# A GNN layer's row fetches: SP takes one tile of 48 by byte addresses, in loops of three ring rounds

## The reference

```python
h = relu(layernorm(x))                                        # 12,500 x 256, the "nodes" below
sender_features = nodes[senders]                              # one row of h for each edge
msg_in = jnp.concatenate([sender_features, edges], axis=-1)   # 256 + 64 columns
messages = msg_in @ W_message
agg = jax.ops.segment_sum(messages, receivers, num_segments=total_nodes)
h1 = _layer_norm(jax.nn.relu(agg) + nodes, ln_aggr_scale, ln_aggr_bias)
nodes_out = _relu_mlp_skip(h1, [mlp_W0, mlp_W1, mlp_W2], [mlp_b0, mlp_b1, mlp_b2])
out = x + _layer_norm(nodes + nodes_out, ln_out_scale, ln_out_bias)
```

## Time and profile before

| | |
|---|---|
| Median of 3 runs (lowest, highest) | 2134.97 us (2129.38, 2136.38) |
| The profiled execution, its span | 2135.35 us, 2133.5 us |
| Busy share of PE, PEld, DVE, ACT, POOL | 75%, 52%, 45%, 19%, 74% |
| Mean granted TensorE clock | 0.905 of full speed |
| Edge loads from SP: number, size, to landing | 206, 256 KB, 6.0 us |

### The profile page before, as it was taken

The page is one execution under the profiler, slowest core; times in us unless marked ns, Lnnn a source line. Parts: engine busy times, 40 slices in busy tenths (PEclk is TensorE's granted clock), DMA queues, the critical chain, the costliest instruction groups (busy, mean ns, idle before and its releaser), DMA issues.

```text
span 2133.5 us, 41823 instructions
## 1 busy us (share of the span) xinstructions
PE 1609.0 (75%) x6722; PEld 1119.5 (52%) x6723; DVE 967.5 (45%) x4162; ACT 408.4 (19%) x1209; POOL 1572.2 (74%) x1645
## 2 busy tenths in 40 slices
PE   0059796697778769769769787878887887878886
PEld 0047574475456557547546555545555554545554
DVE  7866453353344344335335334434343434433445
ACT  5852111121111111111111111111111111111112
POOL 7657777777777777777777777777777777777772
PEclk9989997898888889879889889999999999999988
DMA  9796466556646646655664664665566466566461
GB/s 384 249 247 187 139 174 166 142 163 171 166 135 174 166 137 176 165 152 155 168 165 143 165 169 135 172 166 158 146 173 162 138 168 163 145 165 163 140 188 55
DMA packets 369326, 357.18 MB, mean 167 GB/s; under 512 B 256288, under 2 KB 312672, under 8 KB 369152
## 3 DMA queue, kind: packets, MB, share of 16 engines
q0 software_dynamic: 78576, 214.67, 35.3%
q1 hardware_dynamic: 233984, 89.44, 17.1%
q10 hardware_dynamic: 56592, 51.54, 7.7%
HBM read 329.01 MB, written 26.48 MB: 167 GB/s over the span
## 4 chain that ended last, share of the span: by engine, by line
POOL 42%; SPq 23%; issue 21%; PE 7%; DVE 2%; DMA 2%; ACT 2%; DVEq 0%; POOLq 0%; ACTq 0%
POOL ring L435 42%; SPq L401 16%; SPq L327 4%; PE acc_banks L628 3%; SPq L342 2%; ACT xs L761 1%; SPq L328 1%; PE agg_bank L504 1%; DMA xs<-x 1%; PE agg_bank L509 1%; PE y_bank L492 1%; DVE x_stats L1042 1%; ACT ring L761 1%; PE z_bank L492 1%; POOL xs L447 0%
## 5 line engine op out<-in xcount | busy, mean ns | idle before, releaser
L435 POOL DMA_INDIRECT ring<-h_table,src_all x1557 | 1491.7, 958 | 488.1 <-issue 471.8
L628 PE MATMUL acc_banks<-ring,onehot 128*128 128x320 f32 x3290 | 1027.4, 463 | 330.6 <-DMA ring<-h_table,src_all 161.2
L628 PEld LDWEIGHTS acc_banks<-ring,onehot 128*128 128x128 f32 x3290 | 634.2, 201 | 683.7 <-issue 487.7
L1159 DVE TENSOR_SCALAR onehot<-iota,dst_rel 128x128 f32<-128x128 f32 x1664 | 350.2, 296 | 353.0 <-PE acc_banks L628 325.4
L825 DVE TENSOR_TENSOR visit_rows<-agg_bank,visit_rows 128x256 f32<-128x256 f32 x98 | 41.6, 424 | 722.9 <-PE agg_bank L509 715.2
L678 ACT ACTIVATE uT<-z_bank,fp 128x128 f32<-128x128 f32 x196 | 78.9, 453 | 1266.4 <-PE z_bank L498 1261.5
L504 PE MATMUL agg_bank<-wm,ST 128*128 128x256 f32 (+1 forms) x582 | 172.0, 418 | 0.0
L504 PEld LDWEIGHTS agg_bank<-wm,ST 128*128 128x128 f32 (+1 forms) x582 | 110.7, 203 | 59.6 <-issue 40.0
L498 PE MATMUL z_bank<-ident,z 128*128 128x128 f32 x196 | 41.6, 297 | 104.5 <-DMA ring<-h_table 103.5
L684 ACT ACTIVATE r_bank<-y_bank,fp 128x128 f32<-128x128 f32 x196 | 58.6, 337 | 297.8 <-PE y_bank L492 297.8
L509 PE MATMUL agg_bank<-wl,u 128*128 128x256 f32 x392 | 114.5, 416 | 0.0
(11 more groups left out here) (173 smaller groups left out, 1089.0 us busy)
## 6 DMA issues: line engine op xcount, KB each, us to landing
ring<-edges SPq DMA_DIRECT2D x206, 256.0 KB, 6.0
ring<-h_table SPq DMA_DIRECT2D x3072, 1.0 KB
ring<-h_table,src_all POOLq DMA_INDIRECT x1557
h_in<-h_table ACTq DMA_DIRECT2D x98, 128.0 KB
visit_rows<-h_table ACTq DMA_DIRECT2D x98, 128.0 KB
visit_rows<-x ACTq DMA_DIRECT2D x98, 128.0 KB
out<-o ACTq DMA_DIRECT2D x93, 128.0 KB
xs<-x SPq DMA_DIRECT2D x10, 896.0 KB, 10.8
```

The costliest lines, as they stand in the source:

```text
L435: nc.gpsimd.indirect_dma_start(out=ring[:, k * G + j, 0:D], out_offset=None, in_=rows, in_offset=bass.IndirectOffsetOnAxis(ap=src_all[:, g ...
L628: return nc.tensor.matmul(acc_of(at), onehot[:, hot + j, :], rhs[:, k * G + j, :], start=False, stop=True, skip_group_check=True)
L1159: op = nc.vector.tensor_scalar(onehot[:, ((k + AHEAD) % OG) * G + j, :], iota[:, :], dst_rel[:, bass.ds((g + AHEAD) * G + j, 1)], None, AL ...
```

## The change

Four edits go together.

1. SP fetches one tile of 48, not one of 64. In the middle part every sixth group (`by_sp`: the sixth, twelfth, eighteenth and twenty-fourth of 24) has its last tile fetched by SP. That is 32 tiles (`SP_TILES`), 4096 rows; GpSimd's gathers leave these out.
2. SP's addresses are bytes. `h_table` is seen as a flat run of bytes, and a row is the 1024 bytes from `at[q]`. Before, a row index was multiplied by 256 and by 4 in a fused register instruction ahead of each DMA; now VectorE shifts all 128 x 32 indices once (`byte_addresses`, behind `x_finish`), into `src_bytes`, and SP brings them into `rows_flat` by 32 small DMAs from on-chip memory, where 24 came from HBM.
3. As 24 is a multiple of 6 and 8, the loops of SP and TensorE now hold three rounds (24 groups) and run 8 times, where they held 8 groups and ran 24 times. `MID` stays 24 and `TAIL` 6. The slots of SP's tiles are now the last of ring places 5, 3, 1 and 7 in turn.
4. TensorE waits for a whole tile of SP's rows at once, on two semaphores used in turn, and the counts of `gathered` follow the new pattern.

```diff
@@ -21,6 +22,8 @@
 OG = 4
 PT = 2
 BY_ROW = 32
+SP_EACH = 6
+ROW = 4 * D
 XS = 5
 IN_RING = 4
 AT_ONCE = 6
@@ -47,9 +50,17 @@
     NX = NB // XB
 
     RAWS = RG + EG
-    MID = (NG - RAWS - 1) // RG
+    LOOP = 3 * RG
+    LOOPS = (NG - RAWS - 1) // LOOP
+    MID = LOOPS * 3
     TAIL = NG - RAWS - MID * RG
     LATE = RG - TAIL
+    SP_TILES = MID * RG // SP_EACH
+
+    def by_sp(h):
+        return h % SP_EACH == SP_EACH - 1
+
+    SP_AT = {h % RG: h for h in range(LOOP) if by_sp(h)}
 
     UNITS = []
     for n in range(NX):
@@ -117,13 +128,14 @@
 
         dst_rel = sb("dst_rel", [P, T + AHEAD * G])
         blk = sb("blk", [P, T + 1])
-        xs = sb("xs", [P, XS, XB, D])
+        xs_flat = sb("xs", [P, XS * XB * D + D])
+        xs = xs_flat[:, 0:XS * XB * D].rearrange("p (s b d) -> p s b d", b=XB, d=D)
 
         h_end, x_end, hb_end = xs[:, 2, 0:LAG, :], xs[:, 3, 0:LAG, :], xs[:, 4, 0:LAG, :]
 
-        xs_flat = xs[:, :, :, :].rearrange("p s b d -> p (s b d)")
         extra = xs_flat[:, 0:max(EG, 1) * G * F].rearrange("p (t f) -> p t f", f=F)
-        rows_flat = xs_flat[0:1, 3 * XB * D:3 * XB * D + ROUNDS * P].bitcast(I32)
+        rows_flat = xs_flat[0:1, EG * G * F:EG * G * F + SP_TILES * P].bitcast(I32)
+        src_bytes = sb("src_bytes", [P, SP_TILES], I32)
 
         def staged(n):
             if n >= IN_RING:
@@ -264,7 +275,8 @@
         raw_in = [sem(f"raw_in{k}") for k in range(RAWS)]
         raw_ready = sem("raw_ready")
         row_src_in = sem("row_src_in")
-        rows_in = [sem(f"rows_in{c}") for c in range(P // BY_ROW)]
+        src_bytes_ready = sem("src_bytes_ready")
+        rows_in = [sem(f"rows_in{c}") for c in range(2)]
         gathered = [sem(f"gathered{q}") for q in range(RG * PAIRS)]
         edges_in = [sem(f"edges_in{k}") for k in range(RG)]
         extra_edges_in = [sem(f"extra_edges_in{e}") for e in range(EG)]
@@ -387,24 +399,31 @@
                 sp.wait_ge(h_stored[s], 16 * USES[s])
             for e in range(EG):
                 load_extra_edges(e)
-            for i in range(1, MID + 1):
-                sp.dma_start(row_src[:, i, :], src[0:1, :, i * RT + RT - 1 + EG * G], allow_slow_non_contiguous=True).then_inc(row_src_in, 16)
-            sp.wait_ge(row_src_in, 16 * MID)
+            sp.wait_ge(src_bytes_ready, 1)
+            for n in range(SP_TILES):
+                sp.dma_start(rows_flat[:, n * P:(n + 1) * P], src_bytes[:, n:n + 1],
+                             allow_slow_non_contiguous=True).then_inc(row_src_in, 16)
+            sp.wait_ge(row_src_in, 16 * SP_TILES)
             row_regs = registers(nc.sync, BY_ROW)
-
-            def load_rows(i):
+            h_bytes = h_table.rearrange("r d -> (r d)").bitcast(U8)
+
+            def load_rows(n, slot, landed):
 
                 for c in range(P // BY_ROW):
-                    at = numbers(nc.sync, row_regs, rows_flat, i * P + c * BY_ROW, NB * P - 1)
+                    at = numbers(nc.sync, row_regs, rows_flat, n * P + c * BY_ROW, (NB * P - 1) * ROW)
                     for q in range(BY_ROW):
                         lane_at = c * BY_ROW + q
-                        sp.dma_start(ring[lane_at:lane_at + 1, RT - 1, 0:D], h_table[bass.ds(at[q], 1), :]
-                                     ).then_inc(rows_in[c], 16)
-
-            with nc.Fori(1, MID + 1, engines=[mybir.EngineType.SP], hint_back_edge=True) as i:
-                for k in range(RG):
-                    load_edges(k, i * RG + k + EG, i * RG + k + EG + 1)
-                load_rows(i)
+                        sp.dma_start(ring[lane_at:lane_at + 1, slot, 0:D].bitcast(U8),
+                                     h_bytes[bass.ds(at[q], ROW)].rearrange("(a n) -> a n", a=1)
+                                     ).then_inc(landed, 16)
+
+            with nc.Fori(0, LOOPS, engines=[mybir.EngineType.SP], hint_back_edge=True) as o:
+                for h in range(LOOP):
+                    k = h % RG
+                    load_edges(k, o * LOOP + RAWS + h, o * LOOP + RG + h + EG + 1)
+                    if by_sp(h):
+                        n = h // SP_EACH
+                        load_rows(o * len(SP_AT) + n, k * G + G - 1, rows_in[n % 2])
             sp.dma_start(h_end, h_blocks[:, NB - LAG:NB, :]).then_inc(end_rows_in, 16)
             sp.dma_start(x_end, x_blocks[:, NB - LAG:NB, :]).then_inc(end_rows_in, 16)
             for k in range(TAIL):
@@ -467,7 +486,7 @@
             for g in range(RAWS, NG):
                 k = (g - RAWS) % RG
                 pool.wait_ge(group_free, g + 1 - (EG if g < RAWS + RG else 0))
-                by_row = k == RG - 1 and g < NG - TAIL
+                by_row = by_sp(g - RAWS) and g < NG - TAIL
                 gather(g, k, h_table, landed(k), ENDS if g == NG - 1 else G - 1 if by_row else G)
             pool.wait_ge(tables, 1)
             passes = numbers(nc.gpsimd, registers(nc.gpsimd, 1), whole, 0, NB)[0]
@@ -582,57 +601,62 @@
 
             def group(p, i, k, fetched, tiles=G):
 
-                offset = {"raw": 0, "extra": RG, "SP": EG, "tail": EG, "later": 0}[fetched]
-                g = i * RG + k + offset
+                offset = {"raw": 0, "extra": RG, "middle": RAWS, "tail": RAWS + MID * RG, "later": 0}[fetched]
+                g = i * (LOOP if fetched == "middle" else RG) + k + offset
                 steered = numbers(nc.tensor, regs, steer_flat, g * W, *[1] * G, G - 1, 1, T)
                 closes, visit = steered[CLOSES], floored(nc.tensor, visit_reg, regs[VISIT])
                 hot = (k + offset) % OG * G
                 rhs = extra if fetched == "extra" else ring
-
-                uses = i if fetched in ("SP", "tail") else (p - 1) * ROUNDS + i + 1 + MID + (1 if k < TAIL else 0)
+                slot = k % RG
+
+                if fetched == "middle":
+                    uses = i * 3 + k // RG + 1
+                elif fetched == "tail":
+                    uses = MID + 1
+                else:
+                    uses = (p - 1) * ROUNDS + i + 1 + MID + (1 if k < TAIL else 0)
                 if fetched == "extra":
                     pe.wait_ge(extra_edges_in[k], 16)
                 elif fetched == "raw":
                     pe.wait_ge(edges_in[k], 16)
                 else:
-                    pe.wait_ge(edges_in[k], (uses + 1) * 16)
+                    pe.wait_ge(edges_in[slot], (uses + 1) * 16)
                 pe.wait_ge(onehots, p * NG + g + 1)
                 if fetched in ("raw", "extra"):
                     pe.wait_ge(raw_ready, k + offset + 1)
 
                 def rows_of(j):
 
-                    slot = k * G + j
-                    pair = slot // PT
                     if fetched in ("raw", "extra"):
                         return
-                    if slot == RT - 1 and fetched == "SP":
-                        for c in range(P // BY_ROW):
-                            pe.wait_ge(rows_in[c], uses * (16 * BY_ROW))
+                    pair = slot * PAIRS + j // PT
+                    last = j // PT == PAIRS - 1
+                    if j == G - 1 and fetched == "middle" and by_sp(k):
+                        n = k // SP_EACH
+                        pe.wait_ge(rows_in[n % 2], (i * (len(SP_AT) // 2) + n // 2 + 1) * (16 * P))
+                    if j % PT:
                         return
-                    if slot % PT:
-                        return
-                    if fetched == "SP" and pair == RG * PAIRS - 1:
-                        pe.wait_ge(gathered[pair], uses * (16 * (PT - 1)))
-                        return
-
                     short = 0
-                    if k == TAIL - 1 and fetched != "SP":
+                    if slot == TAIL - 1 and fetched != "middle":
                         short += PT - min(max(ENDS - j, 0), PT)
-                    if pair == RG * PAIRS - 1:
-                        short += MID
-                    pe.wait_ge(gathered[pair], uses * (16 * PT) - short * 16)
+                    if last and slot in SP_AT and fetched == "middle":
+                        first = (k // RG + 1) * PT - (1 if k >= SP_AT[slot] else 0)
+                        pe.wait_ge(gathered[pair], i * (16 * (3 * PT - 1)) + first * 16)
+                    else:
+                        if last and slot in SP_AT:
+                            short += LOOPS
+                        pe.wait_ge(gathered[pair], uses * (16 * PT) - short * 16)
 
                 def tile(j):
                     at = steered[j]
-                    return nc.tensor.matmul(acc_of(at), onehot[:, hot + j, :], rhs[:, k * G + j, :],
+                    return nc.tensor.matmul(acc_of(at), onehot[:, hot + j, :], rhs[:, slot * G + j, :],
                                             start=False, stop=True, skip_group_check=True)
 
                 def close():
                     pe.wait_ge(close_ready, visit + 1)
                     at = steered[AT]
                     sel = steered[VSEL]
```

(18 more changed lines are left out.)

## The result

| | before | after |
|---|---|---|
| Median (lowest, highest) | 2133.77 us (2129.38, 2136.38) | 2220.92 us (2219.05, 2222.53) |
| Profiled execution, span | 2135.35, 2133.5 us | 2222.53, 2221.1 us |
| Ratio to before, 95% interval | | 1.041 (1.040 to 1.043) |
| Mean granted TensorE clock | 0.905 | 0.862 |

What follows compares the result with a forecast made beforehand. GpSimd set the end before; after, SP's issue would: first tile at 241.4 us, 31 periods of 62.3, then 2.0, 42.3 and 26.6, plus 1.85 outside the span, giving 2245 us (range 2150 to 2285).

Steps and rivals of the forecast that it cites:

- The bound: GpSimd and SP feeding TensorE: both nearly full; SP 3.6 to 4.3 us faster per 64 tiles before, 3 us slower after.
- A row: SP's row fetch: without the fused instruction and its gap, the pitch falls from 0.41 to 0.334 us, a 32-row block to 13.78.
- Edge loads and loop end: SP behind a tile's rows: six queued edge loads, fewer loop ends, 7.2 us on average per period.
- The period and the end: SP's period 62.3 us, 31 after the first tile at 241.4; then 2.0, 42.3 and 26.6 us to the span's end.
- The table load: Each of SP's four blocks loads 32 registers in 2.04 us as before; the skill page's floor would give 2125 us in all.
- SP keeping up: Rival: SP's period is 58.4 us or less, GpSimd sets the end and saves ten microseconds, 2125 us; chance 0.13.
- rows are taken no faster than at 0.41: Rival: SP's DMA issue lengthens by what the fused instruction gave up, period 71.8 us, far slower; chance 0.04.
- transfers are the limit and it doesn't matter who issues: Rival: transfers, not issue, bound the kernel, so moving tiles between SP and GpSimd changes nothing, 2135 us; chance 0.02.
- second rival: The rival of SP's row pitch staying at 0.41 us: headed about 2540 us, summed to 2549; chance 0.04.
- SP's index loads: SP's start: 24 loads took 17.66 us, ending 24 us before the sixth edge load's release; 32 take 6 us more, hidden.

Runs made afterwards that it cites:

- e7: Changed kernel's byte addresses and three-round loops, but SP takes one tile of 192 (8 tiles in all): 2151.94 us, ratio 1.008 to the kernel before.
- e8: Changed kernel, but each of SP's row transfers moves 256 of the 1024 bytes: 2224.26 us, ratio 1.042 to the kernel before.
- e11: Changed kernel with a period's six edge loads between the blocks of rows, one SP tile ahead, on a slow-instruction chip: 3580.82 us, ratio 0.994 to the kernel before.
- e6: Changed kernel, unedited, on a chip with slow instructions: 3615.31 us, ratio 1.007 to the kernel before on the same chip (3590 us).

## Why the prediction was right

**The bound.** The step that decided, that both engines stand nearly full and have to be summed one against the other, held. GpSimd's waits for TensorE, forecast as 60 to 100 us and spread over the run, are 68.5 in 19 waits, which is near 31 periods of 61.67 - 59.4 = 2.3 us. e7 and e8 show the two sides: take SP's tiles away and the time is GpSimd's; keep SP's issue and cut its bytes, and the time stays.

**A row.** Forecast 0.334 us; the block of 32 became 13.43 us, not 13.78. The removed instruction took more with it than its 37 ns and one gap of 39: between move and issue and behind them are now about 65 ns in all, where three gaps made 116. So the saving was (16.14 - 13.43) / 31 = 0.087 us, not 0.076. Per period that is 1.4 us in SP's favour, 43 us over 31 periods, the largest error of the sum.

**Edge loads and loop end.** Forecast 7.2 us of a period; 61.67 - 4 x 13.43 = 7.95 are left for them and for blocks slower than those shown, 0.75 more than forecast, 23 us over 31 periods. In the clean period shown, without a loop end, they take 494.35 - 473.95 - 13.43 = 6.97. The lengthening of the later loads, which the sum kept, is there: 1.19, 1.40 and 1.30 us. The two errors have opposite signs: that the period came out within 0.6 us is in part luck. With the edge loads right and the row's error alone the forecast would have been 2245 + 23 = 2268; it would still have been slower.

**The period and the end.** 61.67 us against 62.3, times 31: 19.5 us. SP's first tile ended at 239.7 us instead of 241.4 (its rows start at 188.83 and take 50.89); from SP's last issue to the end of the span were 69.7 us instead of 70.9. Together 22.4, and 0.4 less outside the span: 2243.6 + 1.85 - 22.8 = 2222.6, and the profiled run took 2222.53. The mechanism was right at every step. Two terms were mis-sized: the saving per row, 0.076 us for a measured 0.087, and what lies between the blocks, 7.2 us for 7.95.

**The table load.** At 2.04 us, the median of 128, it is what it was. The Trainium skill, in "DMA: Bandwidth & Descriptors", section "Latency and other measured facts", gives a floor of about 600 ns for such a load. The prediction wrote that the trace disagrees; it doesn't, since 2.04 us for 32 registers lies above a floor. What failed is to take the floor for the price: that would have given a faster kernel.

**The rivals.** SP keeping up would have needed 58.4; the period is 3.3 above it. That rows are taken no faster than at 0.41 is refuted by 13.43 us a block. That transfers are the limit and it doesn't matter who issues is refuted by the result itself, and by e8. Two slips of the prediction change nothing: this second rival's own sum gives 2549, not the 2540 at its head, and SP's index loads ended 28 us before the sixth edge load is issued, not 24 (185.78 - 140.05 - 17.66).

## What to carry to other kernels

Where two issuing engines share one supply, write both periods down for the same number of tiles before moving any: here 59.4 against 62.3, and the sign of the change stood in that line. An engine that the profile doesn't count as busy, since it only issues, can be full: its queue's period, from the chain in order of time, is its busy share. A cheaper step on an engine pays only where that engine sets the pace; spending the saving on more work there needs the saving to be larger than the work (here a tile costs SP about 124 x 0.087 = 10.8 us less, but has GpSimd's 59.4 us to be issued in, where it had its 79.6 for 63 gathers: 20 us less).

## What the runs showed of the hardware

- Transfers of one row by a register's address follow each other on SP in 0.32 us (move 29 ns, issue 225 ns in the median), whether they move 1024 bytes or 256, and nothing pushed back at that rate: of 4096 issues none took more than 378 ns.
- Edge loads of 256 KB issued one behind the other take SP 0.4 us for the first and 1.2 to 1.4 us for the last three of six, in the period shown. One between two blocks of rows takes 0.40 us (e11), and the rows behind it keep 0.32 us.
- On four of the five chips of the experiments SP's instructions came 0.7 us apart in long stretches, and the unedited kernel before took 3535 to 3601 us instead of 2134. The same change measured 1.041 in the comparison and 1.007 on one of these chips (e6). A ratio between two versions with different bounds is a ratio for one kind of chip.
